# Layer 0's attention: splitting work moved between VectorE, GpSimd and ScalarE, context stores later, FFN weights in four transfers

## The reference, cut to what matters

```python
ln_out = _ln(hidden_states, ln_w, ln_b)
q  = _ln(_fp8_linear_pertensor(ln_out, wq,  wq_scale,  q_in_scale))    # 8 groups, 2 heads each, d = 128
k  = _ln(_fp8_linear_pertensor(ln_out, wk,  wk_scale,  k_in_scale))
v  = _fp8_linear_pertensor(ln_out, wv, wv_scale, v_in_scale)
core = _gqa(q, k, v)                                                   # attention to the 256 own tokens
qx = _ln(_fp8_linear_pertensor(ln_out, wqx, wqx_scale, qx_in_scale))
kx, vx = split(cond @ w_kv_x.T);  kx = _ln(kx)                         # cond: the 1601 context tokens
xout = _gqa(qx, kx, vx)                                                # attention to the context
catq = _div_clamp_fp8(concat(core, xout), proj_smooth)
return catq @ wproj.T * (proj_in_scale * proj_w_scale)
```

## Time and profile before

| what | value |
|---|---|
| median of three runs | 1981.2 us (1978.85 to 1993.53) |
| the profiled execution's own time | 1989.39 us |
| its span | 1987.1 us |
| PE busy | 1772.7 us (89%) |
| DVE busy | 1509.7 us (76%) |
| ACT busy | 1399.7 us (70%) |
| POOL busy | 1368.3 us (69%) |
| TensorE's granted clock, mean | 0.953 |

### The profile page before, as it was taken

One profiled execution on the slowest core, in us unless ns is written; L12 is line 12 of the kernel. 1 busy time (PEld: TensorE's weight loads), 2 busy tenths in 40 slices (PEclk: granted clock), 3 DMA queues, 4 the chain that ended last, 5 costly groups with the idle time before them and its releaser, 6 DMA issues. The chain is left out here.

```text
span 1987.1 us, 45376 instructions
## 1 busy us (share of the span) xinstructions
PE 1772.7 (89%) x16789; PEld 1076.7 (54%) x17000; DVE 1509.7 (76%) x3545; ACT 1399.7 (70%) x2285; POOL 1368.3 (69%) x1189
## 2 busy tenths in 40 slices
...
GB/s 151 84 164 172 176 193 187 176 187 190 182 174 187 156 203 207 201 197 191 183 223 199 204 186 181 178 77 1 67 2 2 34 2 2 1 2 2 1 2 22
DMA packets 539531, 245.74 MB, mean 124 GB/s; under 512 B 505392, under 2 KB 512560, under 8 KB 537648
## 3 DMA queue, kind: packets, MB, share of 16 engines
...
...
## 5 line engine op out<-in xcount | busy, mean ns | idle before, releaser
L2436 ACT ACTIVATE P<-score 128x1024 f32<-128x1024 f32 x384 | 373.0, 1022 | 104.0 <-PE score L2522 100.3
L1722 PE MATMUL score<-KK,QT 128*128 128x512 bf16 (+2 forms) x1794 | 321.3, 323 | 32.6 <-DVE mxp L1213 24.8
L1742 PE MATMUL pv<-PT,VV 128*128 128x256 bf16 (+1 forms) x2880 | 338.6, 274 | 5.2 <-DMA PT<-PB 5.0
L2234 POOL TENSOR_TENSOR l_rr<-l_rr,mhalf 128x32 f32<-128x32 f32 (+1 forms) x60 | 329.1, 5485 | 5.0
L1236 DVE SCALAR_TENSOR_TENSOR PB<-S,rsum,PB 128x1024 bf16<-128x1024 f32 (+1 forms) x256 | 317.1, 1239 | 2.6 <-ACT PB L1476 2.5
L1742 PEld LDWEIGHTS pv<-PT,VV 128*128 128x128 bf16 (+1 forms) x2880 | 280.1, 98 | 71.8 <-issue 31.6
L1476 ACT ACTIVATE PB<-S,rsum 128x1024 bf16<-128x1024 f32 (+1 forms) x256 | 246.4, 989 | 101.4 <-DVE rsum L1245 97.1
L2540 PE MATMUL pv<-P,V 128*9 128x256 f32 (+1 forms) x3328 | 266.1, 393 | 13.2 <-ACT P L2436 12.8
L1722 PEld LDWEIGHTS score<-KK,QT 128*128 128x128 bf16 x1920 | 161.2, 99 | 167.9 <-DVE mxp L1213 33.9
L1466 ACT ACTIVATE S<-S,nmx 128x1601 f32<-128x1601 f32 x128 | 209.7, 1638 | 33.4 <-DVE nmx L1227 33.4
L1038 POOL TENSOR_SCALAR S<-S,rsum 128x256 f32<-128x256 f32 x128 | 123.2, 962 | 87.8 <-DVE rsum L1245 86.0
...
## 6 DMA issues: line engine op xcount, KB each, us to landing
...
```

The lines of the kernel that those rows point to most:

```text
L1722: i = e.matmul(m.score[:, at:at + b - a], qt[:, kind, qp, q * P:(q + 1) * P], kk[:, kp, a:b], start=(k == 0), stop=(k == 2))
L1742: i = e.matmul(m.pv[:, at:at + 256], vv[0:rows, v, t, :], m.PT[k % 2][0:rows, turned(c, a), :], start=(c == first and r == 0), stop=(c == ...
L2234: e.tensor_tensor(rr, rr, m.mhalf[0:rows, 0:NH1], ALU.pow).then_inc(s["l1_rr"], 1)
L2436: e.activation(pr[:, :], bank, ACT.Exp, scale=float(D1) ** -0.5).then_inc(s["l1_exp"], 1)
```

## The change

Six edits, all of order or of who does what. The arithmetic is the same.

1. On GpSimd `add_magnitudes` of the last pair of a loop moves behind the next loop's first `query_norm`, in all loops.
2. On GpSimd the split of CVX moves from the end of an even loop to its middle, just ahead of `key_norm`.
3. In odd loops up to 11 the low parts of the own queries Q are written by GpSimd (`pool_queries_low`: per chunk of 128 rows a multiplication by `win` in place, then a subtraction) and no longer by VectorE. For this Q is split ahead of QX, and the counts of the semaphores follow.
4. On ScalarE `exponentials(4 it + 1)` comes ahead of the first context piece, and `query_high(it + 1, 1)` ahead of the others (loops 14 and 19 to 21).
5. The context stores start in loops 6, 10, 15 and 26, where they were in 3, 7, 15 and 24.
6. W1 and W3 come as four transfers of half the size, two in loop 24 and two in loop 25, where they were two transfers in loop 24.

```diff
-    return (QX, K, Q, V) if g < 2 else (V, K, QX, Q)
+    return (QX, K, Q, V) if g < 2 else (V, K, Q, QX)
...
+def pool_queries_low(e, m, s, g):
+
+    c0, width, n = Q
+    out, raw = split_weights(m, g, c0, width), raw_weights(m, g, c0, width)
+    for ic in range(IC):
+        e.wait_ge(s["w_hi"], 8 * g + IC * 2 + ic + 1)
+        e.tensor_scalar(raw[:, ic, :], raw[:, ic, :], m.win[:, n * IC + ic:n * IC + ic + 1], None, ALU.mult).then_inc(
+            s["w_scaled"], 1)
+        e.wait_ge(s["w_scaled"], IC * (g - 2) + ic + 1)
         e.tensor_tensor(out[:, 1, ic, :], raw[:, ic, :], out[:, 0, ic, :], ALU.subtract).then_inc(s["w_lo_pool"], 1)
...
-STORES_AT = (3, 7, 15, 24)
+STORES_AT = (6, 10, 15, 26)
...
-        if it == 3 * G:
-            sp_raw_up(e, m, s)
+        if 3 * G <= it < 3 * G + 2:
+            sp_raw_up(e, m, s, it - 3 * G, 0)
...
         turn_p(4 * it + 1, 1)
+        if 3 * G <= it < 3 * G + 2:
+            sp_raw_up(e, m, s, it - 3 * G, 1)
...
         query_norm(it + 1, 0)
+        add_magnitudes(2 * it - 3)
         take_magnitudes(2 * it - 3)
...
+        if 0 <= it < SPLITS and it % 2 == 0:
+            pool_split_weights(e, m, s, it // 2 + 2, 1)
         for b, i in SPLIT_AT.get(it, ())[0:1]:
             pool_piece_low(e, m, s, b, i)
         key_norm(it + 1)
...
         if 0 <= it < SPLITS and it % 2 == 0:
             pool_split_weights(e, m, s, it // 2 + 2, 0)
+        elif 0 <= it < SPLITS:
+            pool_queries_low(e, m, s, it // 2 + 2)
         magnitudes(2 * it - 1)
-        if 0 <= it < SPLITS and it % 2 == 0:
-            pool_split_weights(e, m, s, it // 2 + 2, 1)
-        add_magnitudes(2 * it - 1)
...
-        if 0 <= it < SPLITS:
-            dve_weights_low(e, m, s, it // 2 + 2, 2 * (it % 2))
+        if 0 <= it < SPLITS and it % 2 == 0:
+            dve_weights_low(e, m, s, it // 2 + 2, 0)
...
+        exponentials(4 * it + 1)
         for b, i in SPLIT_AT.get(it, ())[0:1]:
             act_piece_high(e, m, s, b, i)
-        exponentials(4 * it + 1)
...
+        query_high(it + 1, 1)
         for b, i in SPLIT_AT.get(it, ())[1:]:
             act_piece_high(e, m, s, b, i)
-        query_high(it + 1, 1)
...
-    for k in range(2):
-        e.dma_start(m.raw[k][:, :], raw_parts(m)[k][0]).then_inc(s[f"wp_in{k}"], 16)
+    at = slice(part * WIDE // 2, (part + 1) * WIDE // 2)
+    e.dma_start(m.raw[k][:, at], raw_parts(m)[k][0][:, at]).then_inc(s[f"wp_in{k}"], 16)
```

More of the change, by code:

```diff
@@ L68 @@
 ln_stats ln_aggr ln_eps ln_rs ln_out xw_turned xw_done
-w_hi w_hi_pool w_lo_dve w_lo_pool ctx_hi ctx_lo_dve ctx_lo_pool
+w_hi w_hi_pool w_scaled w_lo_dve w_lo_pool ctx_hi ctx_lo_dve ctx_lo_pool
 xq_scaled xq_step xq_done
@@ L349, in wait_split, with low_before @@
     e.wait_ge(s["w_hi_pool"], 4 * (g + 1))
-    e.wait_ge(s["w_lo_dve"], 8 * g + (4 if keys else 8))
-    e.wait_ge(s["w_lo_pool"], 4 * (g + 1))
+    e.wait_ge(s["w_lo_dve"], low_before(g, 8, 6) + (8 if g < 2 else 4 if keys else 6))
+    e.wait_ge(s["w_lo_pool"], low_before(g, 4, 6) + (4 if g < 2 or keys else 6))
+def low_before(g, first, later):
+    return first * min(g, 2) + later * max(g - 2, 0)
 def wait_stored(e, s, g, keys):
@@ L524, in pool_split_weights @@
         e.wait_ge(s["w_cent"], g + 1)
-        if g >= 2:
-            wait_stored(e, s, g, True)
+    if g >= 2:
+        wait_stored(e, s, g, True)
     for ic in range(IC):
-        n = 4 * g + IC * part + ic
+        n = 4 * g + IC * (part if g < 2 else 1 - part) + ic
         e.tensor_copy(out[:, 0, ic, :], raw[:, ic, :]).then_inc(s["w_hi_pool"], 1)
         e.wait_ge(s["w_hi_pool"], n + 1)
+        e.tensor_tensor(out[:, 1, ic, :], raw[:, ic, :], out[:, 0, ic, :], ALU.subtract).then_inc(s["w_lo_pool"], 1)
+def pool_queries_low(e, m, s, g):
[6 more added lines that the diff above has]
+        e.wait_ge(s["w_scaled"], IC * (g - 2) + ic + 1)
         e.tensor_tensor(out[:, 1, ic, :], raw[:, ic, :], out[:, 0, ic, :], ALU.subtract).then_inc(s["w_lo_pool"], 1)
```

4 lines of the change are left out of this document (2 added, 2 removed).

## The result

The changed kernel takes 1991.3 us (median of 20 runs, 1989.84 to 1998.88), the kernel before in the same comparison 1984.2 us (20 runs, 1973.76 to 1994.81): ratio 1.0047, 95% interval 1.0032 to 1.0063. It is 7 us slower where 27 us of gain were forecast. Its profiled execution took 1997.16 us, with a span of 1995.0.

A forecast was written before the change was run, and what follows sets the result against it. TensorE bounds undisturbed loops at 34.82 us; splitting loops lose to GpSimd's order. Terms 21.5 - 2.4 - 0.5 + 4.5 + 1.0 + 3.0 = 27.1 us off 1981.2 gave 1954 us, range 1938 to 1973.

The forecast's parts named there:

- Edit 1 elsewhere changes nothing where the norm starts as soon as yt ends: Loops outside the splitting ones: no effect, since the order of length up to split_self is the same.
- S - 24.0 over: Excess over the 34.82 us floor when GpSimd's chain to split_self ends S us after the loop's start.
- Odd loops: Odd splitting loops: the 3.5 us query wait shrinks to 0.5 or less; 5.9 over becomes 1.6, gaining 21.5 us.
- Even loops: Even splitting loops: GpSimd's added work makes them 2.7 us over instead of 2.3, losing 2.4 us in six loops.
- 3.5 roughly fits: Even splitting loops: four new GpSimd instructions take 3.5 us, filling 2.05 idle before the norm and 1.17 left by yt.
- second rival: VectorE and GpSimd collide more: even loops 4.4 us over, odd ones 1 us longer; about 1969 us, chance 0.18.
- Loops 14 and 15: Edit 4 lets ScalarE work during its transfer wait: 4.5 us gained of 8.6 excess, bounds 2 and 6.5.
- Loops 19 to 22 and loop 25: ScalarE's reordering gains 1.0 of 3.3 us in the first; split transfers and later stores gain 3 of 4.3 in loop 25.
- The middle of even loops: Edit 2's four small instructions fill a 2.52 us GpSimd gap; cost 0.1 us per loop, 0.5 in all.
- third rival: TensorE waits over 3 us in one piece in even loops and its clock falls there; about 1995 us, chance 0.07.
- price of the clock: Clock loss after a long TensorE wait, taken as some 1.6 to 2 us each time.
- first rival: VectorE's load bounds the splitting loops: a pair takes 71.4 us, 1.8 over; about 1939 us, chance 0.13.

The follow-up runs named there:

- e10: Changed kernel with GpSimd's wpb instruction cut to 8 columns in place of 1024 from the fourteenth call on; one run of 1984.0 us.
- e9: Changed kernel with edit 1 only up to loop 12, the other five edits kept; 1974.4 us, ratio 0.9938.
- e4: Kernel before with edits 4, 5 and 6 alone; 1976.2 us, ratio 0.996.
- e3: Changed kernel with GpSimd's split_self put ahead of yt and catq in all loops; 1989.7 us, ratio 1.0047.
- e5: Kernel before with edits 2, 4, 5, 6, and edit 1 only at the start of odd splitting loops, split_self there ahead of yt and catq; 1959.7 us.
- e6: Kernel before with edits 2, 4, 5 and 6, so neither edit 1 nor edit 3; 1965.9 us, ratio 0.9925.
- e2: Changed kernel with edit 1 undone, all other edits kept; 1976.7 us, ratio 0.9967.
- e1: Kernel before with edit 1 alone; 2002.3 us, ratio 1.0105.
- e8: Kernel before with edit 3 alone; one run of 1998.5 us.

## Why the prediction was wrong

**"Edit 1 elsewhere changes nothing where the norm starts as soon as yt ends": this step failed.** I read that the norm followed `yt` without idle time and took the two for exchangeable. But that the norm started right behind `yt` does not say that it could have started earlier. VectorE's `a_mv` was ready only 0.37 us before `yt` ended. With `yt` behind it, the norm ends at the same T+18.99 and what follows on GpSimd is up to 1.7 us later (`yt` itself 1.2, the rest from `S<-S,rsum`, 1.50 for 0.93). That moves `wpb` onto `yq`, 0.8 us, and leaves 0.64 for the later `split_self` and the smaller meetings around it (e10). Over loops 13 to 30 it is 19.9 us (e9). The instructions up to `split_self` were as long in sum as before; the wait in front of them was new.

**The rule "S - 24.0 over" was too small.** In the changed kernel `split_self` ends at T+24.2 in an undisturbed loop, at T+26.7 in loop 5 and at T+27.1 in loop 4. By the rule that is 0.2, 2.7 and 3.1 over; measured are 1.4, 3.2 and 4.3. The rule follows the chain to TensorE's next scores. It leaves out that VectorE, once late, is late for `t` and `sqs` as well (TensorE waits 0.6 and 0.4 us for them), and that `wpb` moves with the chain.

Forecast and measurement for the thirty loops: 27.1 less, against 9.4 more. The 36.5 between them: 19.9 edit 1 in loops 13 to 30; 13.0 in loops 1 to 12 (18.6 gained in the forecast, 5.6 in fact); 3.7 in the rest of loops 13 to 30 (8.5 gained in the forecast, 4.8 in e9). Of the 5.6, 2.3 lie in loops 1 and 2, where e4 has as much without edits 1 to 3, so the splitting loops 3 to 12 gained 3.4. Outside the attention the two profiled executions differ by 1.5 us.

**Odd loops**: the mechanism was right. The wait for `kn` is down to 0.2, the granted clock is 1.00 over loops 3 to 12 where it was 0.98, the norm starts where I put it. The size was off, 38.0 for 36.4. `split_self` ends at T+26.7 and not T+25.6, because the norm took 2.9 and not 2.3, and `catq` 1.74 and not 1.3, both with a VectorE instruction beside them. TensorE then waits 0.8 to 1.1 us for VectorE to read the scores and 0.2 to 0.4 for `sqs`. I priced collisions for even loops alone. With `split_self` ahead of the two (e3, e5), the loops are at 36.4 to 36.5.

**Even loops**: 39.2 where I forecast 37.5 and named 39 as the sign of being wrong. The four new instructions took 5.0 us instead of 3.5, all of the idle time before the norm and more: the norm starts at T+19.9, 0.7 later than before. I had reasoned that "3.5 roughly fits". Edit 3 costs 11.7 us without edit 1 (e6 against e2), where I had 2.4, and edit 1 alone costs even loops 1.3 (e1), for which I had no term. In even loops this is the second rival in kind and size: it had them 4.4 over, and 39.2 is 4.4 over. It put another 1 us into odd loops, which are 1.6 above the forecast. The Trainium skill, "Perfetto Trace Analysis", section Optimizing Scalar/DVE Operations, says that such a move might not help. Here it did not: edit 3 costs 13.9 us by itself over loops 3 to 12 (e8).

**Edits 1 and 2 together**: I added up their effects on the odd loops without asking what each does alone. Either one gives 2.0 to 2.9 of 3.0 (e1, e2).

**Loops 14 and 15**: 1.6 of the forecast 4.5. Edits 4 to 6 alone give 0.7, with a shorter wait for `sqs` in loop 14 and a new one for `kn` in loop 15. But kernels that don't differ there took 74.5 (e2) to 77.9 (e9), so that the size of this term stays open between 0.4 and 3.7; what makes these loops vary was not tried.

**Loops 19 to 22 and loop 25**: right apart from edit 1. Without it (e4) they gain 0.6 and 4.3, where I had 1.0 and 3.0. The second is in part luck: with the old transfers loop 25 was only 1.0 over in e8 and 0.2 in e1, so that the 4.3 to be gained belong to the one execution that I had read.

**The middle of even loops** cost nothing that shows: e6's even loops are at 37.1.

**The third rival**, which ended at 1995, gave nearly the right time for the wrong reason: TensorE's longest wait in the splitting loops was 1.9 us, and over loops 3 to 12 the granted clock was 1.00. The loops that I took for untouched decided. Its price of the clock was also a wrong sum: 41.07 - 34.82 less 3.5 and 0.6 is 2.15, and not 1.6 to 2. **The first rival**, VectorE's load, had a pair of splitting loops 1.8 over; 38.0 and 39.2 are 7.6 over.
